# Message layer of a graph network: one batch-wide tile of halves, identity sums of 512 columns, the sum over the axes on TensorE, turning back and scan two batches later

## What is computed

```
h      = relu(w1 * edge_weight + b1)                  # 64 hidden values per edge
R      = w2 . h + b2                                  # 6 x 8 x 8 radial weights per edge
f      = features of the source node                  # 8 scalars, 8 vectors of 3
f'_c   = sum_a frame[a, c] * f_a                      # rotated into the edge's frame ("part")
m[u]   = sum_v R[u, v] * f'[v]                        # 32 outputs per edge, each over 2 x 8 values of v
out_i  = sum_a frame[i, a] * m_a[u]                   # rotated back, sum over the three axes a
result = segment_sum(out, dst)                        # by a scan with masks along the edges
```

## Time and profile before

| | |
|---|---|
| device time, median of 3 runs | 5232.38 us (5230.93 to 5241.88) |
| span of the profiled execution | 5108.9 us |
| PE, DVE, ACT, POOL busy | 54%, 57%, 15%, 77% of the span |
| layer 1 (first radial product to last scan) | 2358.6 to 4960 us of the span |
| radial products of a batch (32 passes of 256 columns) in 2000 us of layer 1 | 2436, so 26.3 us a batch |

### The profile page before, as it was taken

One profiled execution on the slowest core, in us unless ns is written; L12 is line 12 of the kernel. 1 busy time (PEld: TensorE's weight loads), 2 busy tenths in 40 slices (PEclk: granted clock), 3 DMA queues, 4 the chain that ended last, 5 costly groups with the idle time before them and its releaser, 6 DMA issues.

```text
span 5108.9 us, 49007 instructions
## 1 busy us (share of the span) xinstructions
PE 2764.0 (54%) x14521; PEld 2489.1 (49%) x14521; DVE 2890.6 (57%) x4976; ACT 754.9 (15%) x1220; POOL 3938.7 (77%) x3539
## 2 busy tenths in 40 slices
PE   0000000000000000025999999999999999999983
PEld 0000000000000000024888888888888888888873
DVE  7333333333333333344777777777777777777765
ACT  1111111111111111100111111111111111111110
POOL 7777777777777777777787787778778778778757
PEclk9999999999999999999999999999999999999995
DMA  3111111111111111111221222222122212212211
GB/s 78 27 26 28 28 27 26 28 28 27 26 28 28 27 26 28 28 23 31 44 43 39 44 44 44 42 44 44 39 44 44 44 42 44 43 40 44 44 31 24
DMA packets 178117, 182.73 MB, mean 36 GB/s; under 512 B 62498, under 2 KB 146101, under 8 KB 171575
## 3 DMA queue, kind: packets, MB, share of 16 engines
q1 hardware_dynamic: 71478, 127.76, 8.9%
q0 software_dynamic: 106624, 54.80, 7.9%
HBM read 119.70 MB, written 62.61 MB: 36 GB/s over the span
## 4 chain that ended last, share of the span: by engine, by line
POOL 50%; PE 20%; issue 20%; DVE 8%; DVEq 0%; DMA 0%; POOLq 0%; ACT 0%; SPq 0%; ACTq 0%
POOL got L453 31%; POOL got L507 16%; PE ps_m L704 12%; PE ps_r L719 4%; PE ps_r L721 2%; DVE prod L1183 2%; DVE halves L1145 2%; PE ps_m L688 1%; POOL back L490 1%; POOL terms L494 1%; DVE prod L1191 1%; DVE part L1165 1%; POOL ngot L478 1%; DVE pick L1077 0%; DVE prod L1100 0%
## 5 line engine op out<-in xcount | busy, mean ns | idle before, releaser
L507 POOL DMA_INDIRECT got<-x_d,idx x1568 | 1849.2, 1179 | 513.5 <-issue 489.7
L453 POOL DMA_INDIRECT got<-in_x_dram,idx x1536 | 1647.5, 1073 | 489.7 <-issue 489.7
L704 PE MATMUL ps_m<-halves,ident 128*128 128x128 f32 x6272 | 1532.3, 413 | 59.9 <-DVE halves L1145 59.9
L704 PEld LDWEIGHTS ps_m<-halves,ident 128*128 128x128 f32 x6272 | 1270.2, 209 | 203.1 <-DVE halves L1145 76.0
L667 PE MATMUL ps_r<-hot_j,hot_p 128*128 128x98 bf16 x1568 | 145.8, 282 | 2000.0 <-DVE hot_j L798 2000.0
L667 PEld LDWEIGHTS ps_r<-hot_j,hot_p 128*128 128x128 bf16 x1568 | 125.0, 141 | 2020.9 <-DVE hot_j L798 1986.3
L719 PE MATMUL ps_r<-wc,hid 128*128 128x256 f32 x3136 | 953.8, 386 | 26.7 <-ACT hid L601 13.6
L988 DVE COPY terms<-runs 128x32 f32<-128x32 f32 x98 | 19.1, 194 | 1322.1 <-issue 682.0
L721 PEld LDWEIGHTS ps_r<-wc,hid 128*128 128x128 f32 x3136 | 600.0, 191 | 85.2
L721 PE MATMUL ps_r<-wc,hid 128*128 128x128 f32 x3136 | 605.8, 275 | 0.0
L993 DVE TENSOR_TENSOR_SCAN runs<-masks,terms 128x544 f32<-128x544 f32 x196 | 258.9, 1321 | 579.4 <-POOL terms L494 576.1
(11 more groups left out here) (134 smaller groups left out, 1637.5 us busy)
## 6 DMA issues: line engine op xcount, KB each, us to landing
run_d<-runs_t SPq DMA_DIRECT2D x196, 256.0 KB
hid<-weight_t SPq DMA_DIRECT2D x98, 512.0 KB, 5.7
got<-x_d,idx POOLq DMA_INDIRECT x1568
got<-in_x_dram,idx POOLq DMA_INDIRECT x1536
frame_d<-frame SPq DMA_DIRECT2D x98, 72.0 KB, 1.6
frame<-frame_d SPq DMA_DIRECT2D x98, 72.0 KB
ngot<-run_d,pos_c POOLq DMA_INDIRECT x196, 2.4
unit<-in_edge_attr_dram SPq DMA_DIRECT2D x1, 2058.0 KB
```

The source lines that it names most:

```text
L453: pool.indirect_dma_start(got[k][:, t, :], None, x, bass.IndirectOffsetOnAxis(ap=(idx_start if first else idx)[k][:, t:t + 1], axis=0)).th ...
L507: pool.indirect_dma_start(got[k][:, t, :], None, x1_d, bass.IndirectOffsetOnAxis(ap=idx[k][:, t:t + 1], axis=0)).then_inc(got2_landed[k], 16)
L704: mm = pe.matmul(ps_m[:, k, g * SG * D:(g + 1) * SG * D], ident[:, :], halves[g % 2][:, :, :, v].rearrange("p t o -> p (t o)"), start=(v = ...
```

## The change

- `halves` becomes a tile for a whole batch (16 edges x 32 outputs x 8 values), one for even batches laid over `unit` (which layer 1 does not use), one for odd batches over the room of `x_sb`. `halve` on DVE writes its quarter after each group as before.
- `add_halves` on PE sums a whole batch: eight products of 512 columns instead of four times eight of 128. They stand one batch later: three of them after the radial weights of group 1, three after group 2, two after group 3.
- The sum over the axes leaves POOL (`add_axes`, two adds, and the constants LAG and BEFORE_ADDS go) and becomes three products of 384 columns with the identity on PE, accumulated in the second bank of `ps_m`; ACT copies the result to `terms` (`vectors`).
- Turning back and scan work on the batch two before, not the one before. Turning back stands on DVE behind the rotation's first products and the last `halve`; since `frame` has been overwritten by then, SP loads it a second time into `frame_b`.
- ACT's order: scalars and masks of b-2 right behind the relu; `vectors`, carry and turned runs of b-2 at the end of the batch. SP's store of the runs moves to batch b-3.

```diff
-        x_sb = sb("x_sb", [P, NPP, D])
+        x_room = sb("x_room", [P, T * D * MUL])
+        x_sb = x_room[:, 0:NPP * D].rearrange("p (j f) -> p j f", f=D)
...
-        halves = [sb(f"halves{k}", [P, SG, D, MUL]) for k in range(2)]
+        halves = [room.rearrange("p (t o v) -> p t o v", o=D, v=MUL) for room in
+                  (unit[:, :, :].rearrange("p t c -> p (t c)")[:, 0:T * D * MUL], x_room[:, :])]
...
# SP
+            def back_frame(b, k):
+                if not isinstance(b, int) or b > 1:
+                    sp.wait_ge(back_ready, b - 1)
+                sp.dma_start(frame_b[k][:, :, :, :].rearrange("p t c a -> p (t c a)"),
+                             frame_rows[:, bass.ds(b * (T * 9), T * 9)]).then_inc(frame_b_loaded[k], 16)
...
# POOL
-            def add_axes(b, k):
-                pool.wait_ge(back_ready, b + 1)
-                pool.tensor_tensor(back[:, 0], back[:, 0], back[:, 1], ALU.add).then_inc(back_step, 1)
...
-                pool.tensor_tensor(terms[k][:, MUL:D, 1:T + 1].rearrange("p (u i) t -> p t i u", i=3),
-                                   back[:, 0], back[:, 2], ALU.add).then_inc(rotated_out, 1)
...
# ACT
+            def vectors(b, k):
+                act.wait_ge(axes_summed, b + 1)
+                act.copy(terms[k][:, MUL:D, 1:T + 1].rearrange("p (u i) t -> p t i u", i=3),
+                         ps_m[:, 1, 0:T * 3 * MUL].rearrange("p (t i u) -> p t i u", i=3, u=MUL)
+                         ).then_inc(rotated_out, 1)
...
# PE
+            def add_halves(b, k, vs):
+                if vs[0] == 0:
+                    pe.wait_ge(halves_ready, GROUPS * (b + 1))
+                    if not isinstance(b, int) or b > 0:
+                        pe.wait_ge(back_ready, b)
+                        pe.wait_ge(m0_copied, b)
+                for v in vs:
+                    mm = pe.matmul(ps_m[:, 0, :], ident[:, :], halves[k][:, :, :, v],
                                    start=(v == 0), stop=(v == MUL - 1))
...
+            def add_axes(b):
+                pe.wait_ge(back_ready, b + 1)
+                if not isinstance(b, int) or b > 0:
+                    pe.wait_ge(rotated_out, b)
+                for a in range(3):
+                    mm = pe.matmul(ps_m[:, 1, 0:T * 3 * MUL], ident[:, :],
+                                   back[:, a].rearrange("p t i u -> p (t i u)"), start=(a == 0), stop=(a == 2))
+                mm.then_inc(axes_summed, 1)
...
+                    radial(b, k, 0)
+                    radial(b, k, 1)
+                    if not isinstance(b, int) or b > 1:
+                        add_axes(b - 2)
+                    if not isinstance(b, int) or b > 0:
+                        add_halves(b - 1, 1 - k, (0, 1, 2))
+                    radial(b, k, 2)
+                    if not isinstance(b, int) or b > 0:
+                        add_halves(b - 1, 1 - k, (3, 4, 5))
+                    radial(b, k, 3)
+                    if not isinstance(b, int) or b > 0:
+                        add_halves(b - 1, 1 - k, (6, 7))
...
# DVE, layer1
-                        halve(b - 1, GROUPS - 1, False)
+                        halve(b - 1, 1 - k, GROUPS - 1)
+                    if not first:
+                        turn_back(b - 2, k)
...
-                        if g == 1 and not (first and k == 0):
-                            turn_back(b - 1, 1 - k)
-                        if g == 2 and not (first and k == 0):
-                            scan2(b - 1, 1 - k)
+                        if g == 2 and not first:
+                            scan2(b - 2, k)
```

More of the change, by code:

```diff
@@ L137, in build_program @@
         frame = [sb(f"frame{k}", [P, T, 3, 3]) for k in range(2)]
+        frame_b = [sb(f"frame_b{k}", [P, T, 3, 3]) for k in range(2)]
         hot_p = [sb(f"hot_p{k}", [P, T, P], BF16) for k in range(2)]
@@ L509, in layer1 @@
                                                 ).then_inc(got2_landed[k], 16)
-                        if t == BEFORE_ADDS and 2 * rounds + k >= LAG:
-                            add_axes(b - LAG, (k + LAG) % 2)
             nodes_in_dram()
             layer1(0, 0)
-            layer1(1, 1)
-            with pool.Fori(2, PAIRS) as i:
-                layer1(i, 2)
-            for b in range(BATCHES - LAG, BATCHES):
-                add_axes(b, b % 2)
+            with pool.Fori(1, PAIRS) as i:
+                layer1(i, 1)
             runs_in_dram(1)
@@ L613, in layer1 @@
                                    scale=-1.0).then_inc(turned_copied, 1)
-                    if not (first and k == 0):
-                        scalars_and_masks(b - 1, 1 - k)
+                    if not isinstance(b, int) or b > 1:
+                        vectors(b - 2, k)
+                        carry_and_turn(b - 2, k)
             act.wait_ge(loaded_net, 64)
-            layer1(0, True)
-            with act.Fori(1, PAIRS) as i:
-                layer1(i, False)
-            carry_and_turn(BATCHES - 2, 0, PAIRS - 1)
-            scalars_and_masks(BATCHES - 1, 1)
-            carry_and_turn(BATCHES - 1, 1, PAIRS - 1)
+            layer1(0)
+            layer1(1)
+            with act.Fori(2, PAIRS) as i:
+                layer1(i)
+            for b in (BATCHES - 2, BATCHES - 1):
+                scalars_and_masks(b, b % 2)
+                vectors(b, b % 2)
+                carry_and_turn(b, b % 2)
             nodes(1)
@@ L1016, in layer0, with loop @@
                         copy_idx(b + 2, k)
-            def loop(body, count):
+            def loop(body, count, peeled=1):
                 s.base, s.n = s.base + s.n, 0
-                body(0, True)
+                for i in range(peeled):
+                    body(i, i == 0)
                 start = s.base + s.n
                 per = STEPS[body.__name__]
-                with dve.Fori(1, count) as i:
-                    s.base, s.n = start + (i - 1) * per, 0
+                with dve.Fori(peeled, count) as i:
+                    s.base, s.n = start + (i - peeled) * per, 0
                     body(i, False)
                     assert s.n == per, (body.__name__, s.n)
-                s.base, s.n = start + (count - 1) * per, 0
+                s.base, s.n = start + (count - peeled) * per, 0
             loop(layer0, PAIRS)
@@ L1137, in turn_back, with halve @@
                 ins.then_inc(back_ready, 1)
[L1139 removed]
+            def halve(b, k, g):
                 q = g % 2
                 dve.wait_ge(multiplied, GROUPS * b + g + 1)
[L1143 to L1146 removed]
+                if g == 0 and (not isinstance(b, int) or b > 1):
+                    dve.wait_ge(summed, b - 1)
+                dve.tensor_tensor(halves[k][:, SG * g:SG * (g + 1)], prod[q][:, :, :, 0:MUL],
+                                  prod[q][:, :, :, MUL:2 * MUL], ALU.add).then_inc(halves_ready, 1)
             def scan2(b, k):
@@ L1187, in layer1 @@
                         if g > 0:
-                            halve(b, g - 1, first and k == 0 and g < 3)
+                            halve(b, k, g - 1)
                         else:
```

140 lines of the change are left out of this document (67 added, 73 removed).

## The result

The changed kernel took **5472.18 us** (median of 4 runs, 5462.77 to 5494.07) beside 5237.13 us of the kernel before: a ratio of **1.046** [1.044, 1.0479]. The forecast was 5254 us and its range ended at 5345. The direction was right, the size was not. To read what follows one fact is needed: the runs were made on several chips, and on some of them signals from one engine to the next (the semaphores at which the engines meet) come some microseconds late now and then, whichever kernel runs; the result above, and the median of 5232.38 us shown ahead of the prediction, are from such chips, the trace ahead of the prediction is not.

What follows compares the result with a forecast made beforehand. POOL was taken as the bound (25.85 us a batch), PE 0.45 us behind. Start, 95 batches at 26.45 us and a 24.5 us tail gave +21.5 us on 5232.4: about 5254 us, range 5215 to 5345.

Steps and rivals of the forecast that it cites:

- What bounds the kernel: Layer 1 loop: POOL sets the usual batch at 25.85 us, PE is 0.45 us behind it.
- POOL's part: POOL in layer 1: without its two adds (2.02 us a batch) it needs 24.27 us with its long gaps.
- PE's sums: PE's sums over halves: sixteen passes of 512 columns at 0.873 us take 13.97 us a batch instead of 14.84.
- rival 3: PE's sums: all of a pass goes by columns, 0.88 us a batch more, 5338 us; chance 0.12.
- a round two beats: PE's sums: 0.213 us for 128 strided columns is two 2.4 GHz beats each, leaving 0.02 us fixed per pass.
- The axes: PE's three added products of 384 columns: six contiguous passes at 0.33 us, 1.97 us a batch.
- DVE, ACT, SP: Other engines in layer 1: their work keeps ahead of PE's need; turning back is covered with some 0.5 us.
- The sum: Whole kernel: start, 95 batches at 26.45 us and tail add 21.5 us to span and median, giving about 5254 us.
- the tail: After PE's last radial batch: last sums, axes, copies, turning back and scan take 24.5 us together.
- The cover: PE's wait at the axes: DVE's chain of 8.2 us against 8.8 on PE covers turning back with some 0.5 us.
- PE, never idle: PE in layer 1: it works without idle time at 26.45 us a batch and keeps granted clock 1.00.
- rival 4: PE waits for turning back: DVE slowed by 1.2 us a batch costs 57 us, 5311 us; chance 0.08.

Runs made afterwards that it cites:

- in a row: Changed kernel, but PE's 512-column sums read adjacent floats instead of every eighth (sum over v not formed): 4792.83 us, 0.9391 of the kernel before.
- step 2: Changed kernel with halves laid out so PE reads every second float, DVE writing pairs: 4800.18 us, 0.9422 of before; with late signals 5224.76 us, 0.9985.
- the run with one axis: Changed kernel with only the first of the three axis products made on PE: 5324.48 us, 1.0118 of the kernel before, on a chip with late signals.

## Why the prediction was wrong

*What bounds the kernel, and POOL's part.* Right. POOL set the batch, and without its adds it needs 23.0 to 23.4 us (24.27 forecast); the runs in a row and with step 2 showed it as the bound.

*PE's sums: the step that failed first.* The prediction took 0.213 us per 128 strided columns and 0.02 as fixed, 0.873 a pass and 13.97 us a batch. Measured are 0.897 for the first pass of a piece and 0.918 for the others, pieces of 5.49, 5.49 and 3.66 us: **14.64 us**, 0.67 more, 0.2 under the sixteen by 128. Hardly anything of the 0.232 was fixed: 0.918 / 4 = 0.2295. It was near rival 3 (0.928, 5338), which had 0.12. The argument against rival 3, "a round two beats", counted for too much: the two beats were right as a picture (0.449 doubles to 0.900), but the remainder belonged to the columns, not to the pass. That sixteen long passes instead of sixty-four short ones would win 0.87 us of PE's batch is what failed; they won 0.2. The error was 5% of one term, and it had 97 repetitions.

*The axes.* Right: 0.32 us a pass, 3006.24 to 3008.18 for six, 1.94 against 1.97. PE's batch is then 4 x 2.63 + 14.64 + 1.94 = 27.1, where 26.45 was forecast.

*DVE, ACT, SP.* Right where signals come in time. PE idles 0.0 us in 2700:4700 of that run. Turning back ends near 3005.3 and the axes start at 3006.24, 0.9 us of cover where 0.5 was counted:

```profile
3003.84 1.47 DVE L1167 TENSOR_TENSOR back<-ps_m,frame_b 128x384 f32<-128x384 f32 x3
...
3006.24 2.10 PE L725 MATMUL ps_m<-back,ident 128*128 128x384 f32 x6
```

*The sum, without late signals.* Forecast span 5130.4, measured 5184.3. The loop is 95 x 0.66 = 63 us longer; the start is 13 us earlier (first axes at 2410.1, not 2423); the tail, from the last sums beside radial work to the end of the scan, is 30.0 instead of 24.5 us. 4 us of that are the axes, which stand alone there, behind a wait:

```profile
5008.89 4.21 PE L725 MATMUL ps_m<-back,ident 128*128 128x384 f32 x6 [2.57 <-DVE back L1167]
5012.89 14.88 PE L715 MATMUL ps_m<-x_room,ident 128*128 128x512 f32 x16
```

The window of that place and of usual axes beside radial work (PE, PEld, DVE, ACT, POOL busy, granted clock, DMA share, GB/s):

```profile
5009.00:5012.80 3.80, 3.80 (x6) 2.07 (x7) 0.00 (x0) 0.00 (x0) 0.00 (x0) 0.50 0.00 0
3006.30:3008.10 1.80, 1.80 (x7) 1.09 (x7) 1.51 (x3) 0.51 (x2) 0.83 (x1) 1.00 0.18 41
```

The granted clock is 0.50 (1.2 GHz) after PE idled, against 1.00 (2.4 GHz), and six contiguous passes take 4.00 us instead of 1.94. The sixteen strided ones behind them start 0.92 us apart throughout, the first three still at 0.50, the others at 1.00. Together 63 - 13 + 5.5 = 55.5 us, where 53.9 is measured. This part alone makes +1.8% out of the +0.4% forecast, and by itself it would have stayed inside the range.

*The cover: the step that failed worst.* The other 2.8% (139 of its some 150 us lie in the loop) come from the sentences "the new wait on turning back is covered with some 0.5 us" and "PE, never idle". The count of the cover was right (0.9 us measured), what it is worth was not: the prediction priced rival 4 as a constant 1.2 us from ports, at 0.08, counted the axes alone and not radial group 1, and did not ask what cover the kernel before had. It had 3.6 us, the changed kernel has 1.0, and in 3 batches of 7 a signal is held some 4 us, of which 3.1 and more reach the end of the batch: 157 us in the loop, against 18.5 in before. That there are late signals at all no row ahead of the prediction showed; the one sign was that the medians stood 123.5 us above the span, which the prediction carried through as "unchanged". And that the changed kernel meets five times as many of them as before could not be foreseen and is not explained.

*Shown and not shown.* Shown: the price of a pass by its step; that PE alone sets 27.1 us; what a forced lateness costs either kernel and where PE waits for it; the split of the loss. Argued from PE's order, and tried in no run: that sums put back between radial groups 0 and 1 would restore the cover. Not shown: what holds the signals, and why one kernel meets more of them than another. Every timed run has a span of its own, so every one was recorded; that the recording itself takes part in the lateness is not excluded.

## What to carry to other kernels

Before lengthening an instruction, ask what its unit cost is made of: if a pass doesn't get faster with the clock, look at the step at which it reads, and change the layout first (two neighbouring floats were enough to halve it here). Two engines that are both nearly full have to be relieved together. When work moves on an engine, count for each wait behind it how late the other engine may be before this one idles, before and after: work taken from between two waits is cover lost, even where the usual batch never touches it. When a time and a span differ by much more than they do in one and the same run (2 us here), they come from different kinds of run, and one is not to be subtracted from the other.

## What the runs showed of the hardware

- A PE pass of 512 f32 columns starts 0.429, 0.449, 0.900, 0.918 us behind the last at steps of 1, 2, 4, 8 floats at a granted clock of 1.00, and 0.853, 0.853, 0.900, 0.918 us at 0.50 (four and five passes for the last two).
- DVE's add of 1024 elements from two SBUF operands takes 1.22 us when it writes singly in a row, in pairs or in fours, and 1.94 us when each float lands 512 floats from the last. An indirect DMA that POOL issues beside nothing but that add takes 1.87 us instead of 0.94 (before, 2700:4700).
- POOL makes a gap of 2 to 4 us in front of every 112th gather of layer 1, in every trace of the unaltered kernel before and of the changed kernel, on chips of both kinds (gathers 2004, 2116, 2228, ...). On chips with late signals the long batches follow the same count: one in seven batches of 16 gathers in the run with one axis, three in seven in the changed kernel.
- Of the five chips of the experiments two delivered signals late in every trace (4 and 5 of them), and three in none; a trace of such a run holds 25,000 to 31,000 semaphore records where the others hold 70,000, so the releasers in it are less sure than the starts. What sets the two kinds of chip apart is open.
